# ScalarE lays out the softmax rows for the scan and makes one of five source one-hots, in a four-layer graph network on one Trainium2 core

## The reference

```
e     = leaky_relu(el[src] + er[dst], 0.2)
emax  = segment_max(e, dst)
ee    = exp(e - emax[dst])
denom = segment_sum(ee, dst)
agg   = segment_sum(feat[src] * (ee / denom[dst])[:, :, None], dst)
```

## Time and profile before

| | us |
|---|---|
| median of 3 runs | 2873.62 |
| the runs | 2870.65 to 2877.45 |
| the profiled execution | 2873.24 |
| its span from first to last instruction | 2871.4 |
| busy in it: PE, DVE, ACT, POOL | 1930.3, 1900.1, 527.7, 1980.3 |
| `gat`: first fence to last gather | 92 to 487 |
| `cheb0`: the same | 626 to 889 |
| `cheb1`: the same | 953 to 1217 |
| `gatv2`: the same | 1319 to 1652 |
| `agnn`: the same | 2488 to 2804 |

### The profile page before, as it was taken

One profiled execution on the slowest core, in us unless ns is written; L12 is line 12 of the kernel. 1 busy time (PEld: TensorE's weight loads), 2 busy tenths in 40 slices (PEclk: granted clock), 3 DMA queues, 4 the chain that ended last, 5 costly groups with the idle time before them and its releaser, 6 DMA issues.

```text
span 2871.4 us, 52037 instructions
## 1 busy us (share of the span) xinstructions
PE 1930.3 (67%) x19915; PEld 1673.4 (58%) x19915; DVE 1900.1 (66%) x4887; ACT 527.7 (18%) x583; POOL 1980.3 (69%) x1825
## 2 busy tenths in 40 slices
PE   2466665449993699842888833378877887269890
PEld 2466665249993699832888811245544554269890
DVE  7599999336562565525888841377777776588885
ACT  0144444112221122210111122000000000011112
POOL 6788886327776677748788830488888886648884
PEclk7788888559996899956999955699999999689995
DMA  6133333112221222213222213211111111313221
GB/s 225 45 98 95 100 98 106 57 32 69 64 68 28 61 69 65 55 23 132 48 58 59 50 38 133 80 46 47 46 47 47 46 47 37 139 37 70 63 49 25
DMA packets 104645, 194.01 MB, mean 68 GB/s; under 512 B 52441, under 2 KB 71713, under 8 KB 100983
## 3 DMA queue, kind: packets, MB, share of 16 engines
q1 hardware_dynamic: 51528, 137.86, 12.9%
q0 software_dynamic: 53024, 54.88, 11.5%
HBM read 107.45 MB, written 85.19 MB: 67 GB/s over the span
## 4 chain that ended last, share of the span: by engine, by line
POOL 34%; issue 14%; DVE 7%; DMA 6%; PE 3%; ACT 1%; POOLq 0%; DVEq 0%; SPq 0%; ACTq 0%
POOL rows L596 15%; POOL edges_d L596 15%; DVE edges_d L1274 2%; DMA tab_y_dram<-edges_d 2%; PE ps L736 2%; POOL starts_dram L599 1%; DMA idx<-cell_dram 1%; POOL fence L682 1%; POOL agg L596 1%; DMA edges_d<-starts_dram 1%; PE ps L875 1%; DMA rows<-tab_cheb_dram,idx 1%; DVE bigT L1317 0%; ACT edges_d L1013 0%; DVE agg L1072 0%
## 5 line engine op out<-in xcount | busy, mean ns | idle before, releaser
L596 POOL DMA_INDIRECT edges_d<-tab_y_dram,idx x425 | 449.7, 1058 | 230.2 <-DMA idx<-cell_dram 113.5
L736 PE MATMUL ps<-nodes,edges_d 125*128 125x160 bf16 x7140 | 500.8, 234 | 101.9 <-DVE edges_d L1072 92.7
L736 PEld LDWEIGHTS ps<-nodes,edges_d 125*128 125x128 bf16 x7140 | 497.8, 98 | 104.9 <-DVE edges_d L1072 93.1
L736 PE MATMUL ps<-nodes,aggn 125*128 125x180 bf16 (+2 forms) x3372 | 376.1, 244 | 200.6 <-DVE rows L1098 200.5
L781 PE MATMUL ps<-edges_d,scan 125*125 125x480 bf16 x1700 | 386.6, 389 | 147.8 <-DVE edges_d L1688 147.8
L596 POOL DMA_INDIRECT rows<-tab_cheb_dram,idx x374 | 409.8, 1096 | 108.8 <-issue 105.7
L736 PE MATMUL ps<-nodes,agg 125*128 125x180 bf16 (+2 forms) x3564 | 337.8, 244 | 166.9 <-DVE rows L1098 101.4
L781 PEld LDWEIGHTS ps<-edges_d,scan 125*125 125x125 bf16 x1700 | 240.9, 144 | 294.0 <-DVE edges_d L1688 120.1
L736 PEld LDWEIGHTS ps<-nodes,aggn 125*128 125x128 bf16 x3372 | 278.0, 101 | 206.3 <-issue 129.0
L1098 DVE COPY_PREDICATED rows<-picks,ps 125x192 f32<-125x192 uint16 (+4 forms) x850 | 342.1, 404 | 84.3 <-issue 22.9
L736 PEld LDWEIGHTS ps<-nodes,agg 125*128 125x128 bf16 x3564 | 285.3, 101 | 171.8 <-DVE rows L1098 78.1
(11 more groups left out here) (320 smaller groups left out, 2808.4 us busy)
## 6 DMA issues: line engine op xcount, KB each, us to landing
src<-srcT_dram SPq DMA_DIRECT2D x68, 427.2 KB
scan_dram<-scan SPq DMA_DIRECT2D x17, 1700.0 KB
scan_dram<-scan SPq DMA_DIRECT2D x34, 425.0 KB
tab_y_dram<-edges_d SPq DMA_DIRECT2D x5, 2812.5 KB
scanD_dram<-scan SPq DMA_DIRECT2D x34, 400.0 KB
edges_d<-starts_dram SPq DMA_DIRECT2D x2, 3408.0 KB, 20.0
starts_dram<-scan SPq DMA_DIRECT2D x2, 3400.0 KB
edges_d<-tab_y_dram,idx POOLq DMA_INDIRECT x425, 2.6
```

What stands on the lines that cost most here:

```text
L596: pool.indirect_dma_start(o, None, table, bass.IndirectOffsetOnAxis(index, 0)).then_inc(s, SLOT)
L736: ins = pe.matmul(columns_ps[:, i, 0:PICKS * w], hots_[b][lot][:, i * NP:i * NP + P], parts_[:, part, at:at + PICKS * w], start=(lot == 0 ...
```

## The change

VectorE makes four of the five one-hots, in all five passes. The fifth is made by ScalarE (`last_hot`) in two instructions, `Square(source lot - 4)` for the last lot of the partition's set (the bias is a new column `last_lot_neg`) and `Relu(1 - that)`, with a wait on its own semaphore between them; those of chunks 0 and 1 ahead of the pass, that of chunk k+2 in step k after the scan's multiplier and ahead of the turning. TensorE and SyncE wait for `last_hot_ready` instead.

In the softmax passes ScalarE copies the rows into the last head's part of the scan buffer in the scan's order, once the second half of the chunk is taken and the gathers have landed, ahead of the exponential. VectorE's product reads that copy and multiplies it with the weights, one instruction per head as before, the last head in place; all three operands now run through memory without a stride. It waits for `rows_flipped` besides the exponential.

```diff
                         if hots_n.n and k == 0:
-                            sp.wait_ge(source_hots_ready, hots_n.at())
+                            sp.wait_ge(last_hot_ready, hots_n.at())
                         if k >= 2:
 
-                            sp.wait_ge(source_hots_ready, hots_n.at(-1))
+                            sp.wait_ge(last_hot_ready, hots_n.at(-1))
...
                     def step(k, b, t0):
-                        pe.wait_ge(source_hots_ready, hots_n.up())
+                        pe.wait_ge(last_hot_ready, hots_n.up())
...
+                def last_hot(k, b, name):
+
+                    if k >= CH:
+                        return
+                    hot = source_hots(name)[b][LOTS - 1]
+                    act.wait_ge(source_hots_ready, dve_hots.up())
+                    nc.scalar.activation(hot, src16[0:NP, b, 0:PE_COLS[name] * NP + PAD], ACT.Square,
+                                         bias=last_lot_neg[:, 0:1]).then_inc(last_hot_begun, 1)
+                    act.wait_ge(last_hot_begun, last_hots.up())
+                    nc.scalar.activation(hot, hot, ACT.Relu, bias=1.0, scale=-1.0).then_inc(last_hot_ready, 1)
...
                     z, keep, n = scan_views(name)
+                    for k in range(2):
+                        last_hot(k, k, name)
 
                     def step(k, b, t0):
-                        gathered[b].up(SLOT * (L - PE_COLS[name]))
+                        act.wait_ge(rows_in[b], gathered[b].up(SLOT * (L - PE_COLS[name])))
+                        act.wait_ge(half_taken, taken.up(2))
+                        r = rows[0:NP, b, 0:L * width].rearrange("p (t w) -> p t w", w=width)
+                        at = (heads - 1) * HG
+                        nc.scalar.activation(z[b][:, at:at + D, :], r[:, :, 0:D].rearrange("p t f -> p f t"),
+                                             ACT.Copy).then_inc(rows_flipped, 1)
                         apply(ACT.Exp, rw[:, b, :, 0:heads, :])
...
                             ACT.Copy).then_inc(keep_ready, 1)
+                        last_hot(k + 2, b, name)
                         to, of, maxima = turn_rows(k, b, C, z[b])
...
                         value.up()
+                        last_hot(k + 2, b, name)
                         to, of, _ = turn_rows(k, b, D, z[b])
...
-                    for lot in range(making["lot"], min(making["lot"] + count, LOTS)):
+                    for lot in range(making["lot"], min(making["lot"] + count, LOTS - 1)):
...
-                        if lot == LOTS - 1:
+                        if lot == LOTS - 2:
                             ins.then_inc(source_hots_ready, 1)
...
                         w = rw[:, b, 1, 0:heads, :]
+                        vec.wait_ge(rows_flipped, flipped.up())
+                        flat = zh[:, heads - 1, 0:D, :]
                         for h in range(heads):
-                            ins = vec.tensor_tensor(zh[:, h, 0:D, :].rearrange("p f t -> p t f"), over(w[:, h, :], D),
-                                                    r[:, :, 0:D], ALU.mult)
+                            ins = vec.tensor_tensor(zh[:, h, 0:D, :], flat, w[:, h, :].unsqueeze(1)
+                                                    .broadcast_to([NP, D, L]), ALU.mult)
```

More of the change, by code:

```diff
@@ L214, in gnn_kernel @@
         lot_f = sb("lot_f", [NP, LOTS])
+        last_lot_neg = sb("last_lot_neg", [NP, 1])
         pick_of = sb("pick_of", [NP, PICKS, T], U16)
@@ L274, in gnn_kernel @@
         source_hots_ready = sem("source_hots_ready")
+        last_hot_ready = sem("last_hot_ready")
+        last_hot_begun = sem("last_hot_begun")
         rows_gathered = sem("rows_gathered")
@@ L283, in gnn_kernel @@
         rows_turned = sem("rows_turned")
+        rows_flipped = sem("rows_flipped")
         scan_stored = [sem("scan_stored0"), sem("scan_stored1")]
@@ L904, in _ @@
                 gathered = [Count(), Count()]
-                filled = Count()
+                filled, taken, dve_hots, last_hots = Count(), Count(), Count(), Count()
+                def last_hot(k, b, name):
[7 more added lines that the diff above has]
+                    nc.scalar.activation(hot, hot, ACT.Relu, bias=1.0, scale=-1.0).then_inc(last_hot_ready, 1)
                 def turn_rows(k, b, C, z):
@@ L935, in softmax_pass @@
                     chunks(act, [(arg, 2), (value, 2), (scanned, 2), (stored[0], SLOT), (stored[1], SLOT),
-                                 (gathered[0], None), (gathered[1], None)], step)
+                                 (gathered[0], None), (gathered[1], None), (taken, 4), (dve_hots, 2), (last_hots, 2)], step)
                     apply(ACT.Exp, cross[:, 0:heads * NP + heads])
@@ L945, in step @@
                         act.wait_ge(rows_filled, filled.up())
+                        taken.up(2)
                         nc.scalar.activation(z[b], rows[0:NP, b, 0:L * D].rearrange("p (t c) -> p c t", c=D),
@@ L956, in sum_pass @@
                     chunks(act, [(arg, 2), (value, 2), (scanned, 2), (stored[0], SLOT), (stored[1], SLOT),
-                                 (gathered[0], None), (gathered[1], None), (filled, 2)], step)
+                                 (gathered[0], None), (gathered[1], None), (filled, 2), (taken, 4), (dve_hots, 2), (last_hots, 2)], step)
                 def layer_norm():
@@ L1058, in _ @@
                 src16_n = [Count(), Count()]
-                making = {"lot": LOTS}
+                making = {"lot": LOTS - 1}
                 def start_hots(k, b, name):
-                    making.update(lot=0 if k < CH else LOTS, b=b, hots=source_hots(name)[b],
+                    making.update(lot=0 if k < CH else LOTS - 1, b=b, hots=source_hots(name)[b],
                                   n=PE_COLS[name] * NP + PAD)
@@ L1151, in _ @@
                 vec.tensor_copy(lot_f[:, :], lot_i[0:NP, :])
+                vec.tensor_scalar(last_lot_neg[:, :], lot_i[0:NP, LOTS - 1:LOTS], -1.0, None, ALU.mult)
                 vec.tensor_scalar(src_f[:, :], src_f[:, :].bitcast(I32), -float(MID), None, ALU.add)\
@@ L1377, in softmax_pass @@
                     chunks(vec, [(gathered[0], None), (gathered[1], None), (own, None), (act_n, 2),
-                                 (kept, 2), (used, 2), (scanned, 2)] + HOT_COUNTS, step)
+                                 (kept, 2), (used, 2), (flipped, 2), (scanned, 2)] + HOT_COUNTS, step)
                     for h in range(heads):
@@ L1493, in layer_norm @@
                         settle()
-                used, kept = Count(), Count()
+                used, kept, flipped = Count(), Count(), Count()
                 tabD = tab[:, :, :].rearrange("p j c -> p (j c)")[0:NP, 0:J * D].rearrange("p (j c) -> p j c", c=D)
```

## The result

The changed kernel takes **2796.27 us** (median of 4 runs, 2793.12 to 2798.72), the kernel before 2872.44 us (median of 4 runs). The ratio is 0.9731, with a 95% interval of 0.9715 to 0.9748: 76 us, 2.7%, faster. The forecast was 2822 us, 51 us faster. The direction was right, the gain half as large again as forecast; the time lies at the lower edge of the range.

A forecast was written before the change was run, and what follows sets the result against it. POOL's gathers, held by VectorE's products, were taken as the bound or 0.8 us from it in every pass. Gains of 33 (`gat`), 7 (`gatv2`), 10 (`agnn`) and 1 us (`cheb`), 51 off 2873.24, gave 2822 us, range 2796 to 2850.

The forecast's parts named there:

- ScalarE's additions hidden: All passes: ScalarE's copy of the rows and its one-hot delay no other engine; nothing counted for them.
- the forecast's last part: List of signs to check, among them `gat` chunks at 21.3 to 22 us; `gat` giving over 48 us means wrong reasoning.
- VectorE's chunk of `gat`, 21.2 us: In `gat`, VectorE's chunk goes from about 24.0 to 21.2 us, as the product gains 2.8 us.
- What POOL gets: Shorter products hold POOL's gathers less: between 0.5 and 2.8 us gained per `gat` chunk, 1.5 taken.
- 4.8 + 2.8 = 7.6: End of `gat`: 4.8 us of slack VectorE no longer needs, plus 2.8 from the last chunk's product behind the last gather.
- a gather cannot finish while a VectorE product runs: Reading of the trace before the change: products hold gathers, costing POOL 3 to 4 us per `gat` chunk.
- `gatv2` and `agnn`: Shorter product lets POOL's gathers through sooner: 7 us in `gatv2`, 10 us in `agnn`, each 0 to 18.
- The fifth one-hot: Its move off VectorE frees 0.4 us per `gat` chunk, not gained there; some 0.6 in passes with 1754 columns.
- The first: Rival: POOL lets go fully, VectorE and ScalarE set the pace everywhere; 84 us gained, 2789; chance 0.14.
- The second: Rival: POOL keeps its time, only slack and pass ends are gained; 15 us, 2858; chance 0.16.
- the third: Rival: the product is slow for another reason and stays at 1.7 us; 2870; chance 0.02.
- The fourth: Rival: slower, ScalarE's copy in `gat` becomes the bound, each us over 1.6 costing 17; 2882; chance 0.02.

The follow-up runs named there:

- a3_old_product: The changed kernel with the strided product of before, ScalarE's copy of the rows and its wait kept but unused: 2862.64 us, ratio 0.9974.
- a2_hot_only: The changed kernel with the strided product of before and no ScalarE copy, so only the fifth one-hot moved to ScalarE: 2861.80 us, ratio 0.9975.
- f1: The kernel with only the one-hot moved, its product walking feature by feature: rows read with a stride, result contiguous: 2865.07 us, ratio 0.9964.
- a1_product_only: The changed kernel with the fifth one-hot back on VectorE, so only the copy and the contiguous product remain: 2799.14 us, ratio 0.9745.
- c1_half_scans: The changed kernel with the scans of the one-head passes cut into two instructions of 17 and 16 features: 2764.07 us, ratio 0.9619.
- d1_copy_twice: The changed kernel with one more ScalarE copy of the rows per chunk, in `gat` alone: 2822.26 us, ratio 0.9833.

## Why the prediction was right in its direction and too small

- **Durations: right.** Product 0.99 us, four in 3.70 (forecast 3.7); the copy 1.73 and 1.65 us, within the 1.6 to 2.0 given; one-hot 3.41 and 2.99 (forecast 3.4 and 2.9).
- **ScalarE's additions hidden: right.** a3_old_product against a2_hot_only shows the copy free where the product is long. TensorE now starts the `cheb` passes behind ScalarE's one-hot, where "for DVE and not for ScalarE" was said (its two waits for L921 there are 98.4 us, the two for VectorE's L1072 were 92.7), but the passes have changed by +0.7 and -1.5 us, as forecast. The copy was not between turning and exponential "without idle time", as the forecast's last part had it: 0.41 us are left.
- **VectorE's chunk of `gat`, 21.2 us: right** (21.1).
- **"What POOL gets" in `gat`: the step that failed.** I took 1.5 us per chunk, which left POOL at 21.7 us and made it the bound. The gathers are held 2.7 us less per chunk, POOL keeps up with VectorE, and the pass gives 48.2 us. That is just over the upper bound of 48 (17 x 2.8), by which the forecast's own last part calls its reasoning wrong. By its terms: from the first fence to the end of the last gather `gat` took 395.1 us and takes 351.5, or 23.2 and 20.7 us per chunk. That is 43.6 us less, where 17 x 1.5 = 25.5 was put, so this term was 18 us too small. The rest of the pass, behind the last gather, gave 4.6 us, where 4.8 + 2.8 = 7.6 was put. Two errors are in the term. First, POOL's chunk is no fixed number: in the kernel before, its fences 2, 3 and 4 stand at

```profile
130.88 0.99 POOL L618 TENSOR_TENSOR fence<-ones 128x1 f32<-128x1 f32 x1
...
159.27 0.21 POOL L618 TENSOR_TENSOR fence<-ones 128x1 f32<-128x1 f32 x1
...
179.91 0.98 POOL L618 TENSOR_TENSOR fence<-ones 128x1 f32<-128x1 f32 x1
```

  28.4 and 20.6 us for equal work, by where the gathers fall between VectorE's instructions: one gather of the first chunk, at 143.01, took 6.92 us. A margin of 0.5 us between POOL's 21.7 and VectorE's 21.2 could not be read from the mean of such numbers. Second, I costed the hold by the product's length, from "a gather cannot finish while a VectorE product runs". The forecast's own example is against it: the gather at 361.26 ended at 362.81, 0.83 us into the second product. So a waiting gather is let in at a boundary and finishes beside the next product. The strided result let gathers miss a third of the boundaries (16 of 48); the contiguous one lets them in at each. At equal length of the product this took the hold from 2.65 us (a2) to 1.4 (f1), and the shorter product took it on to 0.8. Together the hold beside the four products went from 3.0 to 0.8 us, and the other 0.5 us came off the rest.
- **`gatv2` and `agnn`: right mechanism, size too small.** 10.0 and 16.9 us against 7 and 10, within the 0 to 18 given. In a1_product_only the product alone gives 13.2 and 17.4. As a mean over both passes, the gathers beside a single product are held 0.8 us before and 0.2 after, and those beside the scan alone 1.15 and 0.85. Over all gathers of a chunk it is 0.6 us less in `gatv2` (1430 and 1377 ns each) and 0.9 less in `agnn` (1215 and 1135), where 0.3 and 0.5 were taken.
- **The fifth one-hot: small, as forecast.** In `gat` its move is worth 5 to 6 us (a1 against the changed kernel, a2 against before), against the "not gained" of the forecast. In `gatv2` the pass is 3 to 4 us longer with it in both pairs, which is too little to tell from its spread.
- **The rivals.** The first came true in `gat` alone, and there only to within 0.4 us per chunk, as POOL leads in some executions; the scans, named against it, still hold POOL in the other passes, and c1_half_scans took another 35 us out of them. The second fell. So did the third: the product is short. The fourth was near in kind: d1_copy_twice shows each us of ScalarE above the slack costing 17 us, but the slack was not used up. The statement weighed in the forecast (the Trainium skill, "SBUF — State Buffer", section "Who interferes with whom", which marks it as inferred), by which a `tensor_tensor` would not hold descriptor writing, is not borne out here: that instruction in its new form took 2.2 us of hold per chunk off the gathers.

## What to carry to other kernels

Which of two engines with nearly the same time per chunk leads is not read from mean times, since a held engine's time moves with the other's; read it chunk by chunk from how far the one's output lies ahead of the other's use of it, and give the forecast both outcomes. Where GpSimd's gathers run beside VectorE, long VectorE instructions cost more than their own time, and cutting them so that a gather finds a boundary can pay although VectorE's work grows (32 us for two added lines here). And a copy that takes the stride out of an operand for a busy engine is worth an idle engine's 1.7 us, so long as no third queue, such as SyncE's loads behind a store, waits for that engine's later work.

## What the runs showed of the hardware that I had not expected

- VectorE on 800 fp32 elements per partition: 0.99 us with all operands contiguous, 1.6 to 1.7 us with only the rows read with a stride (f1), 1.74 to 1.76 us with the result strided too. The stride of one input is nearly the whole price.
- A gather of GpSimd held by VectorE's four products was served at the next boundary between two instructions in all 135 cases in which their result was contiguous (0 of 33, 32, 29, 11 and 30 missed in f1, a1, after, d1 and c1): it ended at most 0.91 us behind the next one's start. With a strided result and two inputs it missed 16 of 48 (before), 12 of 43 (a2) and 7 of 39 (a3). What in the strided result does that was not tried further.
- One input alone does not free a gather: the one-input instruction with a strided result held one for 3.31 us. No one-input instruction with a contiguous result was tried.
